# One head's K turned on TensorE, blocks of x in rows of 2 KB, stores of x in another order, and first weight sums moved

## What is computed

```
xn = layernorm(x)                                     # x: 4 x 512 x 512
qkv = silu(xn @ w_qkv.T)                              # 16 heads of 128: q, k, v each
per head, block by block (decay by the head's slope):
  o  = (q * q_decay) @ kv + ((q @ k.T) * diag_decay) @ v
  kv = block_decay * kv + (k * k_decay).T @ v
s = (sigmoid(xn @ w_gate.T) * norm_w * rms_normed(o)) @ w_out.T
g = silu(xn * sum(top-8 weights) + top-8 mixture of expert_bias)
out = x + s * g
```

## Time and profile before

| | |
|---|---|
| median of 3 runs | 1072.16 us (1072.03 to 1074.18) |
| the profiled execution | 1071.83 us, its span 1070.0 us |
| TensorE busy | 1043.9 us, 98% of the span |
| VectorE, ScalarE, POOL busy | 633.0, 600.8, 671.5 us (59%, 56%, 63%) |
| mean granted TensorE clock | 0.997 |
| transfers | 112.59 MB, mean 105 GB/s |

### The profile page before, as it was taken

The page is one execution under the profiler, slowest core; times in us unless marked ns, Lnnn a source line. Parts: engine busy times, 40 slices in busy tenths (PEclk is TensorE's granted clock), DMA queues, the critical chain, the costliest instruction groups (busy, mean ns, idle before and its releaser), DMA issues.

```text
span 1070.0 us, 15318 instructions
## 1 busy us (share of the span) xinstructions
PE 1043.9 (98%) x5540; PEld 889.6 (83%) x5540; DVE 633.0 (59%) x1048; ACT 600.8 (56%) x1074; POOL 671.5 (63%) x699
## 2 busy tenths in 40 slices
PE   7999999999999999999989999999999999999997
PEld 6687887888888888788878888888888888888886
DVE  5357556575756666556535675746666575555557
ACT  6666556564655656555534555646556465555543
POOL 6866656575666858668565785755657475665714
PEclk9999999999999999999999999999999999999999
DMA  4333123252444435444653662321334252332235
GB/s 153 80 77 83 46 72 94 59 150 65 117 122 124 105 112 151 110 108 129 244 153 96 175 180 47 87 64 45 94 96 123 67 151 57 75 94 52 70 82 197
DMA packets 214508, 112.59 MB, mean 105 GB/s; under 512 B 175520, under 2 KB 189984, under 8 KB 214432
## 3 DMA queue, kind: packets, MB, share of 16 engines
q1 hardware_dynamic: 198880, 59.68, 23.6%
q10 hardware_dynamic: 15552, 51.93, 14.7%
HBM read 66.47 MB, written 15.73 MB: 77 GB/s over the span
## 4 chain that ended last, share of the span: by engine, by line
PE 89%; POOL 4%; ACT 4%; DVE 1%; DMA 1%; issue 1%; ACTq 0%; SPq 0%; DVEq 0%; POOLq 0%
PE BS L162 8%; PE BS L164 8%; PE BS L163 8%; PE PX L162 5%; PE PX L164 5%; PE BA L162 5%; PE PX L163 5%; PE BA L164 5%; PE BD L162 5%; PE PO L740 5%; PE BA L163 5%; PE BD L164 5%; PE BD L163 5%; PE PS L655 5%; PE PT L704 4%; PE PO L724 4%
## 5 line engine op out<-in xcount | busy, mean ns | idle before, releaser
L480 POOL TENSOR_TENSOR WL<-ST,WH 128x768 fp32r<-128x768 f32 (+1 forms) x128 | 173.3, 1355 | 126.1 <-ACT WH L476 125.8
L480 POOL TENSOR_TENSOR WL<-STG,WH 128x512 fp32r<-128x512 f32 (+1 forms) x128 | 134.2, 1049 | 142.5 <-ACT WH L476 142.5
L162 PE MATMUL BS<-XH,WH 128*128 128x512 f32 x384 | 159.6, 416 | 2.3 <-ACT K L560 1.6
L164 PE MATMUL BS<-XH,WL 128*128 128x512 f32 x384 | 151.2, 394 | 0.0
L163 PE MATMUL BS<-XL,WH 128*128 128x512 f32 x384 | 150.4, 392 | 0.0
L805 DVE TENSOR_TENSOR Y<-Y,PX 128x512 f32<-128x512 f32 x104 | 71.5, 687 | 124.5 <-PE PX L164 124.0
L763 POOL TENSOR_TENSOR SS<-SS,SQ 128x512 f32<-128x512 f32 x60 | 86.8, 1446 | 32.2 <-ACT SQ L755 32.2
L162 PE MATMUL BD<-XH,WH 128*128 128x512 f32 x256 | 103.4, 404 | 1.0 <-DVE XL L414 1.0
L162 PE MATMUL BA<-XH,WH 128*128 128x512 f32 x256 | 102.8, 402 | 0.0
L162 PE MATMUL PX<-OH,GH 128*128 128x512 f32 x244 | 97.1, 398 | 3.4 <-ACT XR L1026 3.4
L164 PE MATMUL BD<-XH,WL 128*128 128x512 f32 x256 | 100.2, 391 | 0.0
(11 more groups left out here) (303 smaller groups left out, 2430.2 us busy)
## 6 DMA issues: line engine op xcount, KB each, us to landing
STG<-in_wp ACTq DMA_DIRECT2D x77, 512.0 KB, 3.8
V<-VB SPq DMA_DIRECT2D x244, 64.0 KB, 2.4
KN<-P SPq DMA_DIRECT2D x240, 48.0 KB, 2.0
XR<-in_x SPq DMA_DIRECT2D x38, 256.0 KB, 3.2
dgd<-XR ACTq DMA_DIRECT2D x16, 256.0 KB, 2.8
dxh<-WT SPq DMA_DIRECT2D x8, 448.0 KB, 3.4
dxl<-XR SPq DMA_DIRECT2D x8, 448.0 KB, 4.3
XH<-dxh ACTq DMA_DIRECT2D x7, 512.0 KB, 5.5
```

The lines of the kernel that those rows point to most:

```text
L162: eng.matmul(o, ah, bh, start=first, stop=False, skip_group_check=skip)
L164: return eng.matmul(o, al, bh, start=False, stop=last, skip_group_check=skip)
L480: a = op("pool", lambda e, dst=dst, src=src: e.tensor_tensor(WL[:, u, dst], src, f32(WH[:, u, dst]), ALU.subtract))
```

## The change

Four edits. The diff is cut to them.

- `dxh` and `dxl` get 16 more columns for each row, which are never used. A block of x then is no longer 4 KB in one piece for a partition but two rows of 2 KB.
- `unit_store` stores the low parts first, and each of the two stores has a semaphore of its own: `U` waits for the low store alone, `UH` for the high one, `x_block` for both. The unit steps of t = 2 and 3 are planned one slot sooner.
- `k_turn_pe` replaces `k_turn` and `k_scale` for head (7, 1, 0): PE transposes K into `PT`, ACT scales from there into `KD`. It stands at slot 224. The head's squares on VectorE and its four moves on SP fall away.
- The first weights are loaded ahead of the tiles of sequence 1; `w_sums(0)` and the first `w_parts(0, ...)` are recorded sooner.

```diff
-        dxh = nc.dram_tensor("dxh", (128, 14, T), F32, kind="Internal").ap()
-        dxl = nc.dram_tensor("dxl", (128, 14, T), F32, kind="Internal").ap()
+        dxh = nc.dram_tensor("dxh", (128, 14, T + GAP), F32, kind="Internal").ap()
+        dxl = nc.dram_tensor("dxl", (128, 14, T + GAP), F32, kind="Internal").ap()
...
+        def k_turn_pe(c, r, b):
+
+            kk = k_at(c, r, b)
+            wait("pe", tk["k", c, r, b], tk["ident"], *tk["pt"])
+
+            def pe(e):
+                for i in range(3):
+                    m = e.transpose(PT[:, chunk(i)], kk[:, chunk(i)], ident[:, :])
+                return m
+            d = op("pe", pe)
+            tk["turned", b] = d
+            tk["k_read", b] = (d, tk.get(("score", b)))
+            h = 2 * (c % NPAIR) + r
+            wait("act", d, tk["ke"], tk["state"])
+            tk["kd"] = op("act", lambda e: e.activation(KD[:, :], PT[:, 0:3 * C], ACT.Copy, scale=KE[:, h:h + 1]))
...
-            dma(s_us, lambda e: e.dma_start(dxh[:, kk::2, s], f32(UH)))
-            d = dma(s_us, lambda e: e.dma_start(dxl[:, kk::2, s], U))
-            xr_free[2] = xr_free[3] = tk["uh_free"] = tk["us"] = d
+            tk["ul_stored"] = xr_free[2] = xr_free[3] = dma(s_ul, lambda e: e.dma_start(dxl[:, kk::2, s], U))
+            tk["uh_free"] = dma(s_uh, lambda e: e.dma_start(dxh[:, kk::2, s], f32(UH)))
...
-            wait("act", tk["us"], free)
+            wait("act", tk["uh_free"], tk["ul_stored"], free)
...
-                    f32(to[:, s, :]), src[:, s, :]), "act")
+                    f32(to[:, s, :]), src[:, s, 0:T]), "act")
...
-                            plan(s + k, f, c, r, b)
+                        if (c, r, b) == (NPAIR - 1, 1, 0) and f in (k_turn, k_scale):
+                            if f is k_scale:
+                                plan(s + k - 1, k_turn_pe, c, r, b)
+                        else:
+                            plan(s + k, f, c, r, b)
...
-                                                         (160, 163, 166, 170, 180), (181, 184, 187, 190, 200))):
+                                                         (160, 163, 166, 169, 179), (180, 183, 186, 189, 199))):
...
+        w_load(0, "sp")
         t1 = [x_tile(1, t) for t in range(4)]
-        for n in range(3):
-            w_load(n, "sp")
+        w_load(1, "sp")
+        w_load(2, "sp")
...
+                w_sums(0)
...
-        w_sums(0)
         for t in range(4):
             first_a(t, banks0[t], d0[t])
+        w_parts(0, (0,))
...
-        w_parts(0, (0,))
         w_parts(0, (1,))
```

More of the change, by code:

```diff
@@ L27 @@
 NXT = 4
+GAP = 16
 X11, X21, X22, XT3, XT1, XT2, XT4 = range(7)
@@ L120, in build @@
         s_xb = [dsem(f"s_xb{i}") for i in range(7)]
-        s_us = dsem("s_us")
+        s_uh = dsem("s_uh")
+        s_ul = dsem("s_ul")
         s_gl = [dsem(f"s_gl{i}") for i in range(NXT)]
```

## The result

| | before | after |
|---|---|---|
| median of 4 runs, us | 1072.57 (1072.03 to 1074.18) | 1060.55 (1060.40 to 1061.68) |
| the profiled execution, its span | 1071.83, 1070.0 | 1060.56, 1058.7 |

The ratio is 0.9888 with a 95% interval of 0.9871 to 0.9905: faster by 1.1%. 1061.2 was predicted, in a range of 1059.5 to 1064.5.

The account below looks back on a forecast made before the run. TensorE, busy 98% of the span, was taken as the bound, so only its waits and clock pay: 1071.83 - 1.8 - 3.4 - 6.3 + 0.1 + 0.2 + 0.2 = 1060.8; at the median 1061.2, range 1059.5 to 1064.5.

Parts of the forecast that it names:

- What bounds the kernel: TensorE is busy 98% of the span, so a change pays only where it waits or its clock falls.
- the two lines of waits: PE's waits: states of a head for KD, 5.5 us; products into PX for ScalarE's copy of U, 3.4 us.
- the 0.5 put down for costs and waits: Added time: 0.1 for ScalarE's queue at slot 189, 0.2 for jitter, 0.2 for the next head's K moves.
- Start, 1.8: First 30 us: earlier weights and sums free POOL at 19.0 instead of 20.9; PE gains 1.8 us.
- the first pair is 0.2 late, and I cost that at nothing: At the start, POOL's sums end at 12.6, 0.2 after 12.41; free, since PE uses the pair's tiles one after the other.
- Steps of x, 3.4: PE's waits of 2.12 us at 430.84 and 1.26 us at 458.10 for the copy of U both go.
- What that move costs, 0.1: At slot 189 K's eviction out of BA ends about 461.5 on ScalarE; PE wants BA about 462.8; cost 0.1 us.
- K turned by TensorE, 6.3: Head (7, 1, 0): 9.59 us from scores to the next product's end becomes 2.96 plus 0.33 for transposes; gain 6.3.
- What is late next, 0.2 and 0.2: At the half, X22 has 1.1 us of slack; 0.2 for jitter, 0.2 for the next head's K moves.
- rival 1: DMA becomes the bound at the half: PE waits up to 2.0 us for X22 or K; 1063.2, chance 0.16.
- shorter rows are no slower: Rows of 2 KB landed 0.65 us apart per 256 KB, rows of 4 KB 3.4 us for two of 512 KB.
- The other rivals: Start gives nothing: 1063.0, chance 0.08; low stores land in 10 us: 1075, 0.03; states wait for a neighbour: 1064.4, 0.05.

## Why the prediction was right, point by point

- **What bounds the kernel**: right. The start and the two lines of waits were the whole gain: 1.60 + 3.38 + 6.35 = 11.3 us, as much as the span lost. That the sum came within 0.3 us of the profiled time is in part luck: the start gave 0.2 less than put down, and the 0.5 put down for costs and waits did not come.
- **Start, 1.8**: 1.60 by the row at 29.20. The weights landed at 2.7 + 4.9 = 7.6, sooner than the 8.6 put down. The step that failed is "the first pair is 0.2 late, and I cost that at nothing". It was 0.65 late (13.06 against 12.41), because sums and normalisation held each other up: two normalisations took 1.81 in place of 1.00. That carried on through VectorE to the second pair, at 16.19 in place of 15.9, and POOL was free at 19.27 in place of 19.0: the 0.2 that is missing. The reason given, that PE uses the pair's tiles one after the other, looked at the tiles and not at VectorE. The kernel with the sums apart agrees that POOL sets the product: its first pair came 0.7 sooner, its POOL was free 0.3 later, and the product was 0.3 later.
- **Steps of x, 3.4**: 3.38, and right for a reason that was told only in part. The prediction named ScalarE's order and the low store side by side. Alone, neither is worth anything that can be measured; the store decides only once the copy comes sooner. It also said of the turn at slot 169 that it had no wait of PE; with the old stores the moved copy makes one (0.79, on KD).
- **What that move costs, 0.1**: the place was wrong. K's eviction out of BA ended with time to spare (456.23 + 0.60 = 456.8; PE wants BA again at 459.88). But the low part of U, which moved with the step, now stands ahead of K's mixing on VectorE (465.27 and 466.27; before, K's mixing was first, at 469.57 and 471.10). That is the wait of 1.23 above, in one of seven profiles. The prediction followed the moved step on ScalarE and SP, and not on VectorE.
- **K turned by TensorE, 6.3**: 6.4. Three transposes took 528.36 - 528.12 = 0.24, against 0.33 put down and 0.83 by the figure of the Trainium skill that was cited (page "TensorE: Matmul & The Clock Gate", section "Part 4: PE-mode transpose"). One transpose does last 0.27 us in the trace, as the page has it, but they overlap: 0.11 from start to start, and 44 took 4.97. So the figure is not the price of one in a batch. The clock's share, 1.5, is shown by the kernel that kept PE busy.
- **What is late next, 0.2 and 0.2**: no wait of PE came, so the profile ended at 1060.56, against 1060.8. The slack, though, was 0.3 us (537.59 - 527.3 - 10.0), not 1.1: the last block took 10.0 us in place of 9.3, and "shorter rows are no slower", read from other transfers, was wrong for it; without padding it took 9.0. In the variants with rows of 2 KB it landed up to 1.9 us later than that, and PE waited up to 1.2 for it. So rival 1 was closer than its size told. The alignment that the Trainium skill's rule spoke of (page "DMA: Bandwidth & Descriptors", section "How a descriptor splits into AXI transactions") made no difference at that block (10.0 and 10.3). It shows in the stores of 512 bytes: 4.7 us against 4.3, a tenth more, where the estimate from the page was an eighth.
- **The other rivals**: the start did give its gain; the low stores, now issued first, landed in 3.5 us (median) and 7.1 at worst, not 10; states waited for no neighbour.

## What to carry to other kernels

Two edits can be worth nothing measurable each and 3.4 us together, when a step waits for the later of two things: try both before either is dropped. Of a step that is moved, follow every instruction on every queue, and also what will then run beside it on the neighbour engine, since of two that start within 0.01 us of each other either may be held up. When a wait is taken away, work out the slack of the next one (here 0.3 us on a transfer): it says how much of any further gain will arrive.

## What the runs showed of the hardware

- VectorE and GpSimd hold each other up. A low part of 128x896 took 1.09 us or 2.25, and the sum beside it 2.24 or 1.29; normalisations beside sums took 0.94 and 0.95 us each against 0.55 alone. The Trainium skill, page "SBUF — State Buffer", section "Who interferes with whom", says that the two share a pair of ports under an exclusive lock, that an instruction of VectorE with two inputs in SBUF contends with one of GpSimd that reads SBUF, and that the order of issue decides who is blocked. Low part and sum agree with that where their starts lie 0.1 us apart or more (483.14 and 483.28); at 0.01 us the recorded order does not tell. The normalisations agree less well: three sums and two normalisations, about 3.2 us one after the other (an estimate from 0.7 and 0.55 us each), were through in 2.5.
- A wait of 4.87 us was followed by the lower clock until 3.8 us after its end, worth 1.5 us. In the four other profiles with a wait of 4.8 to 5.3 us the granted clock fell to 0.50 within the wait and stayed there until 4.0 to 4.9 us after it, worth 1.9 us (4.01 us from states to the next product, 2.1 at the higher clock). A wait of 2.1 us was followed by it in one profile (1.2 us) and not in four others. PE kept busy with 44 transposes kept 1.00.
- The last block of x at the half landed about 1 us later in rows of 2 KB than in pieces of 4 KB (9.9 to 11.9 against 8.8 to 9.5); the block issued 6 us sooner did not (8.9 to 10.0 against 9.1 to 9.5). Rows of 2 KB let other transfers be issued sooner beside them (4.0 to 4.9 us against 6.35 to 7.81 for four moves of V).
- Stores in pieces of 512 bytes landed in 4.6 to 4.7 us at a pitch of 2112 bytes and in 4.3 at pitches of 2048 and 2304.
